# Six inverse standard deviations of a two-layer graph network: made by one power on GpSimd each instead of ScalarE's root and VectorE's reciprocal

## The reference

```
h  = layer_norm(x, g1, b1)                  # normalisation 1
q, k, v = h@Wq+bq, h@Wk+bk, h@Wv+bv
agg = softmax over the edges of each node of (q[dst].k[src]/4), times v[src], summed at dst
y  = x + agg@Wo + bo
h  = layer_norm(y, g2, b2)                  # normalisation 2
x  = _layernorm(x + y + gelu(h@W1+bf1)@W2+bf2)      # normalisation 3, no weights

q, k, v = x@Wq+bq, ...;  k, v get the edge's features edge_attr@We added
conv = agg + x@Wskip + bskip
h  = _ln(conv + x, g1, b1)                  # normalisation 4
h2 = _ln(gelu(h@Wf1+bf1)@Wf2+bf2 + h, g2, b2)       # normalisation 5
out = _layernorm(x + h2)                    # normalisation 6
```

## Time and profile before

| what | before |
|---|---|
| device time, median of 3 runs | 1789.74 us (1785.43 to 1793.72) |
| span of the profiled execution, first to last instruction | 1423.2 us |
| time of the profiled execution around its span | not recorded; median less span is 366.5 us |
| TensorE busy | 75% of the span |
| VectorE busy | 76% |
| ScalarE busy | 59% |
| GpSimd busy | 63% |
| mean granted TensorE clock | 0.829 |

### The profile page before, as it was taken

The page is one execution under the profiler, slowest core; times in us unless marked ns, Lnnn a source line. Parts: engine busy times, 40 slices in busy tenths (PEclk is TensorE's granted clock), DMA queues, the critical chain, the costliest instruction groups (busy, mean ns, idle before and its releaser), DMA issues. The chain is left out here.

```text
span 1423.2 us, 28503 instructions
## 1 busy us (share of the span) xinstructions
PE 1072.8 (75%) x6809; PEld 956.7 (67%) x6809; DVE 1076.5 (76%) x2695; ACT 840.3 (59%) x2605; POOL 901.0 (63%) x1028
## 2 busy tenths in 40 slices
PE   3937678767877787768896788888888888887790
PEld 1436677667866776758735677787787778776690
DVE  5538877787877787865443888988988898897557
ACT  1615776676667666644443467766776676576351
POOL 2177777777777777531046777777777777770453
PEclk9967877787777777778897989999999999898795
DMA  5385555555555565420024567667766766671001
GB/s 157 106 182 178 173 188 194 191 155 189 193 186 159 192 193 171 137 91 0 7 79 141 176 211 223 197 193 220 214 199 196 224 207 189 219 229 48 1 1 45
DMA packets 100659, 222.50 MB, mean 156 GB/s; under 512 B 34875, under 2 KB 49882, under 8 KB 96941
## 3 DMA queue, kind: packets, MB, share of 16 engines
q0 software_dynamic: 39936, 109.11, 26.8%
q1 hardware_dynamic: 57927, 109.78, 22.8%
q10 hardware_dynamic: 2662, 2.05, 0.5%
HBM read 184.86 MB, written 36.00 MB: 155 GB/s over the span
## 5 line engine op out<-in xcount | busy, mean ns | idle before, releaser
L464 POOL DMA_INDIRECT KV<-kv_table,idx x832 | 810.3, 974 | 301.5 <-issue 247.4
L732 PE MATMUL PS<-QT,OHT 128*128 x1664 | 401.6, 330 | 146.5 <-DVE OHT L990 122.3
L732 PEld LDWEIGHTS PS<-QT,OHT 128*128 128x128 f32 x1664 | 317.9, 236 | 166.1 <-issue 164.6
L733 PE MATMUL PS<-QT,OHT 128*128 x1664 | 390.4, 324 | 0.0
L733 PEld LDWEIGHTS PS<-QT,OHT 128*128 128x128 f32 x1664 | 319.1, 238 | 0.0
L592 ACT ACTIVATE AGG<-AGG,PC,RCS x800 | 309.3, 387 | 3.1 <-ACT AGG L588 2.4
L1008 DVE TENSOR_TENSOR PR<-KV,PS 128x512 f32<-128x512 f32 x208 | 140.6, 676 | 105.6 <-DMA KV<-kv_table,idx 103.7
L778 PE MATMUL PS<-OH,KV 128*128 128x128 f32 x1600 | 208.4, 280 | 2.9 <-DVE OH L1110 1.2
L588 ACT ACTIVATE AGG<-PS 128x127 f32 x800 | 208.0, 260 | 1.0 <-issue 0.7
L778 PEld LDWEIGHTS PS<-OH,KV 128*128 128x128 f32 x1600 | 196.7, 197 | 5.6 <-issue 2.6
L584 ACT ACTIVATE PC<-PS 128x4 f32<-128x4 f32 x200 | 33.5, 168 | 267.1 <-PE PS L778 256.0
(11 more groups left out here) (158 smaller groups left out, 1352.2 us busy)
## 6 DMA issues: line engine op xcount, KB each, us to landing
REL<-rel_dram SPq DMA_DIRECT2D x52, 512.0 KB, 4.4
window_dram<-OH SPq DMA_DIRECT2D x25, 1024.0 KB
OH<-window_dram SPq DMA_DIRECT2D x50, 512.0 KB, 6.1
KV<-kv_table,idx POOLq DMA_INDIRECT x832
EA<-in_edge_batch SPq DMA_DIRECT2D x52, 256.0 KB
kv_table<-KV SPq DMA_DIRECT2D x52, 128.0 KB, 1.7
X<-in_x SPq DMA_DIRECT2D x2, 832.0 KB, 10.1
GATES<-edge_gates SPq DMA_DIRECT2D x8, 208.0 KB, 10.0
```

What stands on the lines that cost most here:

```text
L464: g.indirect_dma_start(KV[:, s, j, :], None, kv_table, bass.IndirectOffsetOnAxis(ap=idx[:, s, j:j + 1], axis=0)).then_inc(gathered[s][hh], 16)
L732: te.matmul(o, OHT[:, q // 2, 0, e0:e0 + P], QT[:, ds(blk, P)], start=True, stop=False)
L733: last = te.matmul(o, OHT[:, q // 2, 1, e0:e0 + P], QT[:, ds(blk + P, P)], start=False, stop=True)
```

## The change

The variance is turned into the inverse standard deviation by one instruction, `RS ** -0.5`, on GpSimd: `inverse_roots(n)` waits for `var_ready` and raises `rs_ready`. The exponent is a constant tile of 128 by 26. `roots` on ScalarE, with its calls of `warm` and its root, and the reciprocal on VectorE are gone. GpSimd's six calls are put into its list in program order. With one step fewer in `moment_step`, its counts fall from 7 to 6 per call.

```
+        minus_half = sb("minus_half", [P, NB])
+            g.memset(minus_half[:, :], -0.5).then_inc(S["half_made"], 1)

+            def inverse_roots(n):
+                pool.wait_ge(*done("var_ready", n))
+                g.tensor_tensor(RS[:, :], RS[:, :], minus_half[:, :], ALU.pow).then_inc(S["rs_ready"], 1)
+
+            pool.wait_ge(*done("half_made", 1))
+            inverse_roots(1)
             pool.wait_ge(S["weights_loaded"], 16 * WEIGHTS)
             g.tensor_tensor(FB[:, 1, :], FB[:, 1, :], GB[:, 1, :], ALU.add)
...
                         g.tensor_tensor(x3, x3, FB[:, 0, :]..., ALU.add)       # end of the additions of layer 1
+                    inverse_roots(2)
+                    inverse_roots(3)
                 else:
+                    inverse_roots(4)
...
                     blocks(pool, affine)
+                    inverse_roots(5)
...
                     blocks(pool, scale_last)
+                    inverse_roots(6)

-            def roots(n):
-                warm(ACT.Sqrt)
-                act.wait_ge(*done("var_ready", n))
-                sc.activation(SD[:, :], RS[:, :], ACT.Sqrt).then_inc(S["sd_ready"], 1)
-                if l == 0:
-                    roots(1)
-                roots(2 if l == 0 else 4)
-                roots(3 if l == 0 else 5)
-            roots(6)

-                dve.wait_ge(*done("moment_step", 7 * n - 1))
-                v.tensor_tensor(RS[:, :], RS[:, :], SD[:, :], ALU.add).then_inc(S["moment_step"], 1)
-                dve.wait_ge(*done("moment_step", 7 * n))
-                dve.sem_inc(S["var_ready"], 1)
-                dve.wait_ge(*done("sd_ready", n))
-                v.reciprocal(RS[:, :], SD[:, :]).then_inc(S["rs_ready"], 1)
+                dve.wait_ge(*done("moment_step", 6 * n))
+                v.tensor_tensor(RS[:, :], RS[:, :], SD[:, :], ALU.add).then_inc(S["var_ready"], 1)
                 dve.wait_ge(*done("rs_ready", n))
```

More of the change, by code:

```diff
@@ L176, in build @@
         counts = """we_zeroed consts_made rel_made gate_made prep_step kv_copied kv_free gates_made loops_step seen_step iota_kept
-            pool_go sp_go stat_step moment_step var_ready sd_ready rs_ready
+            pool_go sp_go stat_step moment_step var_ready half_made rs_ready
             xn_ready tp_ready ht_ready proj_ready q_made x_kept
@@ L883, in inv_std @@
                 v.tensor_tensor(RS[:, :], BN[:, :, 2], BN[:, :, 5], ALU.add).then_inc(S["moment_step"], 1)
-                dve.wait_ge(*done("moment_step", 7 * n - 4))
+                dve.wait_ge(*done("moment_step", 6 * n - 3))
                 v.tensor_scalar(MEAN[:, :], MEAN[:, :], 0.5, None, ALU.mult).then_inc(S["moment_step"], 1)
```

## The result

| | before | after |
|---|---|---|
| device time, median | 1791.08 us (1785.43 to 1793.72, 4 runs) | 1821.95 us (1814.17 to 1829.0, 4 runs) |
| the same two kernels in a later comparison | 1425.99 us (1421.75 to 1432.47, 17 runs) | 1451.5 us (1443.57 to 1458.4, 6 runs) |
| ratio after to before, 95% interval | | 1.0177 (1.0136 to 1.0218); again 1.0176 (1.0142 to 1.021) |

The change makes the kernel 1.8% slower. By the medians that is 30.9 us in the first comparison and 25.5 us in the second (25.1 by its ratio). I had forecast 9.9 us more, and 1820 as the upper end of the range; 1821.95 lies 2 us above it.

A forecast was written before the change was run, and what follows sets the result against it. No engine was near its limit, so chains bound the kernel. -4.5 (stretches) + 0.6 (hand-overs) + 0.56 (queue) + 1.28 (table load) + six powers at 2.0 us made +9.9 us, forecasting 1799.6 us, range 1788 to 1820.

The forecast's parts named there:

- p = 2.0 us: Assumed price of one 128x26 power on GpSimd, chosen between bounds of 0.24 and 25.3 us.
- 6p - 2.1: Forecast change in time over the six normalisations: six powers' price less 2.1 us, giving +9.9 us.
- The 33 steps: Author's own count of steps per column in a GpSimd power, each at an addition's 2.11 ns: 1.81 us.
- p outside 1 to 4 us: Sign that the forecast is wrong: one GpSimd power's duration falls outside 1 to 4 us.
- the 2.97 us: Longest single arithmetic or filling instruction on GpSimd, used as an upper row for the power's price; would give +15.7 us.
- What goes, 4.5 us: Six stretches from variance to first use of the inverse deviations, with root, reciprocal and hand-overs, vanish: 4.5 us together.
- Hand-overs, 0.1 us: VectorE to GpSimd and back at each normalisation: 0.1 us for both, 0.6 us over six.
- The queue, 0.56 us: At normalisation 2 the power waits behind GpSimd's 14 additions: 0.56 us more, once.
- The exposed table load, 1.28 us: ScalarE's first table load moves directly ahead of the first `turned`, with TensorE waiting: 1.28 us more.
- Tables off the path, 0: Five ScalarE table loads that go were all hidden behind waits, so their removal gains 0.
- 1423.2 + 366.5 us: Profiled span of the kernel before plus the time assumed around it, the median less the span, kept unchanged.
- rival (b): GpSimd power made element by element at the gather's price: 25 us each, +150 us, 1939 us; chance 0.10 including lower values above 4 us.

The follow-up runs named there:

- e2: Changed kernel with a multiplication in place of the power, same tiles and waits; ratio to the kernel before 1.0023.
- e4: Kernel before with five extra powers of widths 1, 13, 26, 52 and 26 on GpSimd scratch tiles, where nobody waits; 1430.88 us, one run.
- e1: Kernel before, run again without an edit for a second profile; 1428.8 us, ratio 1.000.
- e5: Changed kernel, run again without an edit, beside the kernel before on the same chip; 1451.5 us, ratio 1.0176.
- e3: Changed kernel with the exponential's table loaded early, right behind the weights' transfers; 1448.22 us, ratio to the kernel before 1.0161.
- e7: Changed kernel with early table load and the powers of normalisations 1 to 5 cut into three pieces; 1441.83 us, ratio to the kernel before 1.0111.
- e8: Kernel before with GpSimd's last six additions held until normalisation 2's inverse deviations are made; 1423.04 us, ratio 0.9983.

## Why the prediction was wrong, by its steps

- **The step that failed: "I take p = 2.0 us".** The formula 6p - 2.1 was right and its p was not. With the measured 4.50 us it gives 24.9 us; the second comparison measured 25.1 (20.2 to 29.9). The 33 steps at an addition's 2.11 ns a column had no row behind their number, and no run shows such steps; the 160 ns a column would be 76 of them. The forecast's own sign of being wrong, p outside 1 to 4 us, has come true. Of the bounds, the 2.97 us (the longest single instruction on GpSimd) was no bound at all for another operation: I treated a coincidence of this kernel as a ceiling. The Trainium skill's page cited beside it (GPSIMD Engine Reference, section Instruction dispatch: an elementwise instruction there is a loop of software) pointed to the right side. The trace agrees that a power can't be had at an addition's price: 0.24 us in e2 and 4.48 us in e4 for one shape.
- **The range:** p = 4.50 alone doesn't leave it. It gives 1789.74 + 24.9 = 1814.6 us, and the range went to 1820. The measured median is 7.3 us higher: 1.3 us of that is the median of before with a fourth run, and the other 6 us are those that no run explains.
- **What goes, 4.5 us:** right; e1 reads 0.75 to 0.77 at each place.
- **Hand-overs, 0.1 us for the two of a site:** right at sites 3 to 6 (4.60 - 4.50), 0.19 at normalisation 1 (24.33 to 24.48, 28.98 to 29.02).
- **The queue, 0.56 us:** right where the kernel before passes late. From the common mark e5 is 22.17 - 17.79 = 4.38 us behind e1, 0.5 more than an ordinary site's 3.84. Against e4, which passes early, it is 22.17 - 15.64 = 6.53, so the queue costs 2.7 us. It is no constant but what VectorE was early, and that the forecast's 0.56 fits e1 and after is in part luck.
- **The exposed table load, 1.28 us:** right to 0.01 us (e3). The drain of 1.38 us that the Trainium skill adds to a load (ScalarE: Activation LUTs, section What ACT_TABLE_LOAD costs) was not seen: putting the load ahead of its wait moved the projection by the load alone.
- **Tables off the path, 0:** right, as far as e2's interval tells. **The rest as before:** right, as far as the rounds' scatter of some 10 us lets one see.
- **Where the time was put:** 1423.2 + 366.5 us. The lump was an artefact of two levels of execution. Because it was added again behind the sum, it did the forecast no harm; but an offset of a fifth of the time should have been read as a profile of another execution than the timed ones.
- **Chances:** rival (b), which held everything above 4 us, had 0.10. That rested on the 2.97 us as a ceiling; without it the rows left everything between 0.24 and 25.3 us open, and 0.10 was too little.

## What to carry to other kernels

An operation that the trace doesn't show has to be measured, or carried with the whole width of its bounds; the cost of an addition of the same shape says nothing of a power, which took 19 times as long. Where all blocks pass through one small instruction, its length counts fully and once for each passage, and the engine's low busy share is no comfort. When such an instruction moves, look at what its new engine has queued ahead of it (it takes away any lead of the old one), and at what its old engine prepared early for it (here a table load that fell onto the path).

## What the runs showed of the hardware

- A power on GpSimd of f32: 160 ns a column of 128 partitions and about 0.3 us of start (e4, e7); 4.50 us for 128x26 (e5), against 0.24 for a product of the same shape (e2).
- VectorE's instructions of 0.2 us take up to 1.3 us beside GpSimd's two-input additions; holding six additions back by 1.8 us (they begin 12.51 us after the mark in e8, 10.69 in e1) made the kernel before 0.17% faster (0.02 to 0.32).
- After the rounds TensorE's clock rose to full for good between 4.4 and 12.4 us after the first output matmul, within the same work.
- The kernel before took 1426 to 1427 us on three chips and 1791 us in the first comparison, whose chip is not on record. The changed kernel's profile at the longer level moved its data at a mean of 122 GB/s against 154 in e5, and its engines stood idle for up to 41 us in the rounds without a releaser in the profile. Why is open.
